# State space chunks of a four-layer attention stack: the skip D x as products with diagonal matrices

## The reference

```
zxbcdt = rms(x) @ in_proj_w              # 1288 columns: z 512, xBC 768, dt 8
xBC = silu(conv4(xBC))                   # x 512 (8 heads of 64), B 128, C 128
dt = softplus(dt + dt_bias);  decay = exp(dt * -exp(A_log))
h_t = h_{t-1} * decay + (dt x)_t B_t     # per head a state of 64 x 128
y_t = h_t C_t
y = ys + D_skip[head] * xh               # the skip D x
u = rms(y * silu(z)) * gnorm_w
x = x + u @ out_proj_w                   # then cross attention on the context
```

## Time and profile before

| | |
|---|---|
| median of three executions | 1053.94 us (1051.53 to 1053.95) |
| profiled execution, its own time | 1055.05 us |
| its span, first to last instruction | 1053.3 us |
| mean granted TensorE clock | 0.904 of full speed |
| TensorE busy | 897.5 us, 85% |
| VectorE busy | 523.1 us, 50% |
| ScalarE busy | 463.6 us, 44% |
| GpSimd busy | 46.2 us, 4% |
| the state space steps | 770 to 819 us and 876 to 925 us of the span |

### The profile page before, as it was taken

The page is one execution under the profiler, slowest core; times in us unless marked ns, Lnnn a source line. Parts: engine busy times, 40 slices in busy tenths (PEclk is TensorE's granted clock), DMA queues, the critical chain, the costliest instruction groups (busy, mean ns, idle before and its releaser), DMA issues.

```text
span 1053.3 us, 11140 instructions
## 1 busy us (share of the span) xinstructions
PE 897.5 (85%) x4450; PEld 420.3 (40%) x4452; DVE 523.1 (50%) x750; ACT 463.6 (44%) x691; POOL 46.2 (4%) x39
## 2 busy tenths in 40 slices
PE   3986799979899989977599998999679997977977
PEld 2533344443344334354223536334246444633332
DVE  3377999832202230254714326249739493954352
ACT  3454222344412431164153343466676477623434
POOL 0000000200000000001300000000012001200000
PEclk9899899979899889976879897899789998998999
DMA  9000000000000000020000000000000000000001
GB/s 370 1 1 0 1 0 0 0 2 1 0 1 1 1 1 0 16 103 1 1 0 1 2 1 1 1 0 1 1 0 1 1 0 1 1 0 1 21 20 40
DMA packets 3003, 15.58 MB, mean 15 GB/s; under 512 B 656, under 2 KB 912, under 8 KB 2320
## 3 DMA queue, kind: packets, MB, share of 16 engines
q1 hardware_dynamic: 2816, 12.88, 3.1%
q0 software_dynamic: 144, 2.10, 0.5%
HBM read 12.87 MB, written 2.10 MB: 14 GB/s over the span
## 4 chain that ended last, share of the span: by engine, by line
PE 58%; DVE 24%; ACT 10%; issue 5%; DMA 1%; DVEq 0%; POOLq 0%; SPq 0%; POOL 0%; ACTq 0%
PE ps L390 56%; DVE AR L1598 2%; DVE AR L1599 2%; ACT AR L598 2%; DVE VB L609 2%; DVE AR L1601 2%; DVE AR L1723 2%; DVE AR L1827 1%; DMA CX<-in_ctxT 1%; DVE AR L1885 1%; DVE AR L479 1%; DVE AR L1892 1%; DVE AR L1888 1%; DVE AR L487 1%; DVE AR L1880 1%
## 5 line engine op out<-in xcount | busy, mean ns | idle before, releaser
L390 PE MATMUL ps<-AR,WA 128*128 128x512 f32 (+3 forms) x808 | 358.9, 609 | 16.6 <-DVE AR L487 6.1
L390 PEld LDWEIGHTS ps<-AR,WA 128*128 128x128 f32 (+2 forms) x808 | 152.4, 194 | 216.0 <-issue 191.0
L390 PE MATMUL ps<-AR,CN 128*128 128x512 f32 (+3 forms) x336 | 132.3, 654 | 33.3 <-DVE AR L482 19.2
L390 PE MATMUL ps<-AR 128*64 128x128 f32 (+4 forms) x684 | 104.5, 443 | 11.8 <-ACT AR L1484 6.2
L390 PEld LDWEIGHTS ps<-AR,CN 128*128 128x128 f32 (+2 forms) x336 | 45.7, 178 | 95.3 <-issue 50.3
L390 PEld LDWEIGHTS ps<-AR 128*64 128x64 f32 (+4 forms) x684 | 54.3, 173 | 57.1 <-issue 18.3
L617 DVE TENSOR_TENSOR AR<-ps,AR 128x512 f32<-128x512 f32 x24 | 16.6, 692 | 120.8 <-ACT AR L603 120.8
L598 ACT ACTIVATE AR<-ps 77x2048 f32<-77x2048 f32 x24 | 44.2, 1871 | 62.7 <-PE ps L390 62.5
L609 DVE TENSOR_REDUCE VB<-ps 128x16 f32<-128x1232 f32 x32 | 45.0, 1439 | 45.5 <-PE ps L390 45.5
L1664 DVE SCALAR_TENSOR_TENSOR X<-ps,VC,X 128x512 f32 x8 | 5.6, 746 | 108.8 <-PE ps L390 108.8
L1324 ACT ACTIVATE AR<-ps,VC 128x512 f32<-128x512 f32 x32 | 22.0, 687 | 80.7 <-PE ps L390 80.7
(11 more groups left out here) (284 smaller groups left out, 1055.8 us busy)
## 6 DMA issues: line engine op xcount, KB each, us to landing
WA<-in_m SPq DMA_DIRECT2D x1, 2856.0 KB, 10.6
WA<-in_m SPq DMA_DIRECT2D x1, 2560.0 KB, 16.2
X<-in_xT POOLq DMA_DIRECT2D x1, 2048.0 KB, 9.9
WA<-in_m SPq DMA_DIRECT2D x1, 2048.0 KB, 21.1
out<-X SPq DMA_DIRECT2D x4, 512.0 KB, 3.1
WB<-in_m SPq DMA_DIRECT2D x1, 1024.0 KB, 22.9
AR<-in_rows SPq DMA_DIRECT2D x1, 640.0 KB, 10.6
WA<-in_m SPq DMA_DIRECT2D x1, 512.0 KB, 17.0
```

The lines of the kernel that those rows point to most:

```text
L390: return nc.tensor.matmul(out, lhsT, rhs, start=first, stop=last)
```

## The change

The four VectorE instructions at L1892 go. In their place GpSimd builds once, after the third layer, four diagonal matrices DIAG in a part of the weight tile WA that the last layer's weights don't use: the identity times the four columns of D_skip. In each piece s3 TensorE now multiplies, for each of the four chunks of features, first that diagonal matrix by the chunk of x in CV (128 output rows), and then accumulates the two heads of the chunk (64 output rows each) on top of it in the same bank. The first product starts the accumulation, so the heads' products no longer do. The waits for the zeroed states, on TensorE and ScalarE, now count four more.

```diff
+        skip_at = sizes[1]
+        DIAG = WA[:, skip_at:skip_at + 4 * P].rearrange("p (c n) -> p c n", c=4)
+        assert skip_at + 4 * P <= sizes[0]
@@ gpsimd, after the memsets of STATE
+            for c in range(4):
+                nc.gpsimd.tensor_scalar(DIAG[:, c, :], cn("ident"), v("dskip", c), None, ALU.mult).then_inc(sem("m0"), 1)
@@ tensor, piece s2, first step (and the same on scalar, piece s1)
-                        pe.wait_ge(sem("m0"), B)
+                        pe.wait_ge(sem("m0"), B + 4)
@@ tensor, piece s3
                     pe.wait_ge(*after(of("dm", b), n + 1))
-                    for h in range(HM):
-                        last = mm(bank(b, 2)[PD * (h % 2):PD * (h % 2) + PD, h // 2 * P:(h // 2 + 1) * P], XT[b][:, h * PD:(h + 1) * PD], DM[b][:, h, :])
+                    for c in range(4):
+                        mm(bank(b, 2)[:, c * P:(c + 1) * P], DIAG[:, c, :], CV[b][:, c, sub], True, False)
+                        for half in range(2):
+                            h = 2 * c + half
+                            last = mm(bank(b, 2)[PD * half:PD * half + PD, c * P:(c + 1) * P], XT[b][:, h * PD:(h + 1) * PD], DM[b][:, h, :], False, True)
                     last.then_inc(sem(of("y1_mm", b)), 1)
@@ vector, piece s3
                     dve.wait_ge(*after(of("yr", b), n + 1))
-                    for c in range(4):
-                        yc = YT[b][:, c * P:(c + 1) * P]
-                        ins = STT(out=yc, in0=CV[b][:, c, sub], scalar=v("dskip", c), in1=yc, op0=ALU.mult, op1=ALU.add)
-                    ch.link(ins)
                     TT(ZF[b][:, :, sub], c3d(YT[b]), ZF[b][:, :, sub], ALU.mult).then_inc(sem(of("y7", b)), 1)
```

More of the change, by code:

```diff
@@ L1472, in _ @@
                     else:
-                        act.wait_ge(sem("m0"), B)
+                        act.wait_ge(sem("m0"), B + 4)
                     for h in range(HM):
```

## The result

| | before | changed |
|---|---|---|
| median | 1053.43 us (1051.53 to 1053.95, 4 runs) | 1083.26 us (1081.84 to 1083.99, 4 runs) |
| profiled execution, own time and span | 1055.05, 1053.3 us | 1081.84, 1080.1 us |
| mean granted clock | 0.904 | 0.908 |

The ratio is 1.0283, with a 95% interval of 1.0269 to 1.0296: 29.8 us slower by the medians.

The account below looks back on a forecast made before the run. It took VectorE's path and an equally long ScalarE-TensorE loop to bound the step. Longer s3 products add 24.4 us in six steps and 4.4 in two fourth steps: +28.8, 1083 us, full range 1068 to 1096.

Parts of the forecast that it names:

- What bounds the kernel: State space block's step: loop through ScalarE and TensorE is as long as VectorE's path, 10.16 us, within about 0.1.
- Rival A: VectorE alone binds, as the chain of waits reads: 8 x 1.17 = 9.4 us go, 1044.5 us; 4 in 100.
- What goes: Removing VectorE's L1892 wins nothing in six of eight steps; 1.17 us at each half's fourth if TensorE were free.
- The price of a chunk: In pieces s3 on TensorE: 0.77 us per chunk with width changes and uncovered loads; 6.06 us for both pieces against 1.99.
- On the path: s1 of batch 0 starts 4.07 us later in six steps, 24.4; out 2.18 later at two fourth steps, 4.4.
- On GpSimd: Building the four diagonal matrices: about 1.04 us, within GpSimd's idle 61.55 us before its first s1, costed at nothing.
- B: TensorE's changes of width cost nothing, 1062 us, or half, some 1073 us; 12 in 100.
- C: TensorE's granted clock falls in s3: 1104 us, or 1090 to 1095 if in a few steps only; 12 in 100.

Follow-up runs that it names:

- e3: Kernel before without VectorE's four skip instructions and nothing in their place, so D x is left out of the result; 1048.91 us, ratio 0.9964.
- e10: Kernel before, skip still on VectorE, with ScalarE's state scaling of batch 1 moved behind the exponential of batch 1; 1052.79 us, ratio 0.9996.
- e4: Changed kernel with VectorE's four skip instructions put back, so the skip is added twice; 1082.28 us, ratio 1.0285.
- e2: Changed kernel with each diagonal product split into two of 64 output rows, so no product in s3 is full width; 1062.30 us, ratio 1.0077.
- e1: Changed kernel with the four diagonal products of each piece s3 put first, then the eight heads; 1066.82 us, ratio 1.0130.
- e5: Kernel before, skip on VectorE, with a full-width product of one column ahead of each pair of heads in s3; 1083.94 us, ratio 1.0297.
- e11: Changed kernel with ScalarE's state scaling of batch 1 moved behind the exponential of batch 1; 1075.67 us, ratio 1.0217.
- e6: Kernel before with ScalarE's order changed alone: state scalings of both batches first in piece s1 of batch 0; 1066.75 us, ratio 1.0130.
- e9: Kernel before with both state scalings first on ScalarE, the skip on GpSimd and VectorE's gate product one instruction later; 1061.58 us, ratio 1.0077.

## Why the prediction was right

Predicted 1083 us, measured 1083.26. The mechanism is the predicted one. That the totals agree within 0.3 us is luck: the block became 30.0 us longer in the traces, not 28.8, while the median before was 1053.43 in the four runs of the comparison instead of the 1053.94 I had started from. By its steps:

- **What bounds the kernel.** The claim that a loop through ScalarE and TensorE is as long as VectorE's path, within 0.1 us, was the hinge: 10.16 us (e3) and 10.11 (e10). The chain of waits had shown one of two. Rival A, 9.4 us less from the same rows, is refuted by e3 and e4.
- **What goes.** Nothing in six steps, 1.17 us at each fourth: e3 has 0.00 and 1.18.
- **The price of a chunk.** 0.77 predicted, 0.79 measured: 0.42 for the diagonal product and 0.37 for the heads, instead of 0.41 and 0.36. Both pieces s3 take 6.19 us, not 6.06, and so end 4.20 us later, not 4.07. The terms were right in kind and size: a narrow pair 0.109 (e2), a change with its uncovered load 0.17 on average (e1), where the sum had 0.09 + 0.05 to narrow and 0.09 + 0.10 to full. The Trainium skill says in "TensorEngine Tiling (Array Packing)", Key Properties, that a change of tiling mode drains TensorE; e1 and e5 agree with it in that every change was paid for. What the engine does meanwhile the traces don't show.
- **On the path.** The 6.31 us from s1 to s2 of batch 1 stayed. At the fourth steps it was 2.31 instead of 2.18. With these sizes the sum of 28.8 becomes 29.8; the first interval of the second half adds the 0.2 up to 30.0.
- **On GpSimd.** The four products took 3.17 us, not about 1: mis-sized by a factor of three, in a bound that the sum didn't use. It was priced from a tensor_tensor of 512 columns, while the kernel before has the same kind of instruction, tensor_scalar: 128x1024 in 3.23 us (L696), of which 512 columns would be 1.6. So each of the four, at 0.79 us, also cost twice its share of the long one. They were done at 716.29 us, 56 us before ScalarE's first scaling (772.10), the first instruction that waits for them.
- **Rivals B and C.** The changes were paid in full. The clock stayed at 1.00 in the changed kernel's steps; in e5 it fell in the same order of widths, with products of one column instead of 128.

VectorE was expected to be busy 7.5 us in a step, and was 7.96.

## What to carry to other kernels

Before work is moved off the engine that the chain names, look for a second loop of the same length, and price the place to which the work goes by what its neighbours there are: a full-width product put between narrow ones cost 0.57 us here, of which 0.22 were its passes. Where products of two widths must stand in one piece, group them; that alone brought back 16 of 30 us. And an engine's slack in busy time is no slack if the step is a loop: here GpSimd's was paid for by VectorE, ScalarE's by the first step. Not run, and so open, is the narrow form of the diagonal products (e2) together with ScalarE's scaling last (e11).

## What the runs showed of the hardware

- A one-column fp32 product between narrow ones takes 0.47 us of TensorE's time, nearly as much as one of 128 columns (0.57); both figures include the changes of width before and behind it.
- Behind eight such one-column products in a step the granted clock fell from 2.4 to 1.2 GHz in two of three steps of e5's first half, for 3.4 and 6.8 us, although the profile counts TensorE as busy all through the stretches ahead (busy 1.00 of 1.00 us in each from 784 to 787 and from 797 to 801). With 128 columns in the same order of widths it stayed at 2.4 GHz in these steps.
- GpSimd and VectorE lengthen each other's instructions when both work from the core's memory, and here the one that started second was the longer. VectorE's 128x512 gate product took 1.49 to 1.51 instead of 0.69 us when it started 0.1 us behind GpSimd's product (e6, e9), which kept its 1.04. In the kernel before the gate product started first, at 787.65, and kept its 0.69, while GpSimd's product from 787.88 took 1.37; in e10 it took 1.38 in the median.
